# The second layer's bias of a mixture of experts: one stacked fp32r product a tile instead of a fp32 product, in two banks and two halves

## What is computed

```python
logits = xf @ gate_w + gate_b
top_v, top_i = jax.lax.top_k(logits, TOP_K)
top_w = jax.nn.softmax(top_v, axis=-1)
cw = jnp.zeros((T, NUM_EXPERTS)).at[jnp.arange(T)[:, None], top_i].add(top_w)
for e in range(NUM_EXPERTS):
    h = jax.nn.relu(xf @ w1[e] + b1[e])
    y = h @ w2[e] + b2[e]
    out = out + cw[:, e:e + 1] * y
```

## Time and profile before

| what | value |
|---|---|
| median of three runs | 1293.33 us |
| the profiled execution | 1289.2 us |
| its span | 1287.5 us |
| mean granted clock of PE | 0.988 |
| PE busy / PEld busy | 1246.4 / 1161.5 us |
| DVE busy / ACT busy / POOL busy | 842.4 / 675.0 / 159.2 us |
| the eight instructions of L1161 | 979.1 to 982.75 us |

### The profile page before, as it was taken

One profiled execution on the slowest core, in us unless ns is written; L12 is line 12 of the kernel. 1 busy time (PEld: TensorE's weight loads), 2 busy tenths in 40 slices (PEclk: granted clock), 3 DMA queues, 4 the chain that ended last, 5 costly groups with the idle time before them and its releaser, 6 DMA issues.

```text
span 1287.5 us, 22172 instructions
## 1 busy us (share of the span) xinstructions
PE 1246.4 (97%) x8497; PEld 1161.5 (90%) x8497; DVE 842.4 (65%) x2186; ACT 675.0 (52%) x1193; POOL 159.2 (12%) x86
## 2 busy tenths in 40 slices
PE   7999999999999999999999999999878999999997
PEld 6799999999999999999999999988767988989996
DVE  4556656566565666556566566685576788877877
ACT  5345545535544553464455455354444676767673
POOL 2203101300400220040031013000021000000012
PEclk9999999999999999999999999999969999999999
DMA  9002200310220040022022003100226667677763
GB/s 329 27 1 88 82 1 1 118 52 1 91 79 2 27 142 1 1 91 79 2 90 80 1 7 143 38 2 7 97 74 241 226 240 254 238 240 250 230 220 114
DMA packets 61506, 129.04 MB, mean 100 GB/s; under 512 B 3572, under 2 KB 21120, under 8 KB 61160
## 3 DMA queue, kind: packets, MB, share of 16 engines
q1 hardware_dynamic: 59240, 120.85, 27.4%
q0 software_dynamic: 2176, 6.95, 1.6%
HBM read 121.89 MB, written 15.34 MB: 107 GB/s over the span
## 4 chain that ended last, share of the span: by engine, by line
PE 92%; DVE 4%; ACT 2%; DMA 1%; issue 1%; POOL 0%; SPq 0%; POOLq 0%; DVEq 0%
PE ptp L830 24%; PE work L830 20%; PE work L1128 8%; PE pv L975 7%; PE ptp L959 7%; PE work L868 6%; PE work L1130 4%; PE ptp L1149 2%; PE ptp L1152 2%; PE ptp L1151 2%; PE ptp L1153 2%; PE ptp L1150 2%; PE work L837 2%; PE ptp L837 1%; DVE pt L1379 1%; DMA raw<-in_ctxT 1%
## 5 line engine op out<-in xcount | busy, mean ns | idle before, releaser
L830 PE MATMUL ptp<-vw_hi,cx_hi 128*128 128x256 f32 x832 | 241.8, 291 | 0.0
L830 PE MATMUL ptp<-vw_lo,cx_hi 128*128 128x256 f32 x832 | 235.4, 283 | 0.0
L830 PE MATMUL ptp<-vw_hi,cx_lo 128*128 128x256 f32 x832 | 235.4, 283 | 0.0
L518 POOL TENSOR_TENSOR cx_lo<-raw,cx_hi 128x1664 fp32r<-128x1664 f32 x30 | 113.8, 3792 | 666.3 <-ACT cx_hi L578 666.3
L830 PE MATMUL work<-cx_hi,kw_hi 128*128 128x400 f32 (+1 forms) x504 | 175.5, 348 | 2.9 <-POOL cx_lo L518 1.7
L830 PEld LDWEIGHTS ptp<-vw_hi,cx_hi 128*128 128x128 f32 x832 | 159.3, 191 | 17.0 <-issue 17.0
L830 PE MATMUL work<-cx_hi,kw_lo 128*128 128x400 f32 (+1 forms) x504 | 173.6, 345 | 0.0
L830 PE MATMUL work<-cx_lo,kw_hi 128*128 128x400 f32 (+1 forms) x504 | 173.2, 344 | 0.0
L1379 DVE TENSOR_TENSOR pt<-ptp,pt 128x512 fp32r<-128x512 f32 (+1 forms) x224 | 141.3, 650 | 33.3 <-ACT pt L578 29.8
L830 PEld LDWEIGHTS ptp<-vw_lo,cx_hi 128*128 128x128 f32 x832 | 159.3, 191 | 0.0
L830 PEld LDWEIGHTS ptp<-vw_hi,cx_lo 128*128 128x128 f32 x832 | 159.3, 191 | 0.0
(11 more groups left out here) (268 smaller groups left out, 2384.9 us busy)
## 6 DMA issues: line engine op xcount, KB each, us to landing
w1raw<-in_w SPq DMA_DIRECT2D x32, 1024.0 KB, 5.1
w2raw<-in_w SPq DMA_DIRECT2D x32, 1024.0 KB, 6.9
raw<-in_ctxT SPq DMA_DIRECT2D x31, 832.0 KB, 6.3
pr<-in_mask SPq DMA_DIRECT2D x8, 800.5 KB, 4.4
xrow<-x_rows SPq DMA_DIRECT2D x7, 256.0 KB, 6.2
y_rows<-y_out_rows POOLq DMA_DIRECT2D x7, 256.0 KB, 2.4
xin<-in_x SPq DMA_DIRECT2D x1, 1024.0 KB, 8.9
qwraw<-in_qwT SPq DMA_DIRECT2D x1, 1024.0 KB, 11.1
```

The lines of the kernel that those rows point to most:

```text
L518: pool.tensor_tensor(cx[1][:, :, sl], raw[:, k % 2], cx[0][:, :, sl].bitcast(F32), ALU.subtract).then_inc(c_lo, 1)
L830: last = pe.matmul(dst, lhs(i, c), rhs(j, c), start=(c == 0 and (i, j) == (0, 0)), stop=(c == n - 1 and (i, j) == (1, 0)))
```

## The change

`b2s` and `cwT` become fp32r and get 96 rows instead of 8. Three groups of 8 rows are used, at rows 0, 32 and 64; the others meet zeros in `cwT`. The weights side is high, low, high (of `cw`), the bias side high, high, low (of `b2`), so one product over 96 rows gives high x high + low x high + high x low.

For this b2 is loaded twelve times (into 96 rows), ACT makes the high part of all 96 rows, and DVE replaces rows 64 to 71 by the low part. DVE splits `cw` into `cw_k` (128 tokens x 96, zeroed by POOL), which PE turns instead of `cw`. The four products go by turns into `yb[2]` and `yb[3]`, two ahead of `second(0, 0, 0)` and two behind it, and `second(0, 0, 0)` no longer waits for `y_out`; the wait for all four additions is in front of piece 2, where `yb[2]` and `yb[3]` are used again.

```diff
+BK = 96
+B_HI, B_LO, B_HI2 = slice(0, E), slice(32, 32 + E), slice(64, 64 + E)
-            sp.dma_start(b2s[:], b2).then_inc(ld2[5], 16)
+            for i in range(BK // E):
+                sp.dma_start(b2raw[i * E:(i + 1) * E, :], b2).then_inc(ld2[5], 16)
+            pool.memset(cw_k[:], 0.0).then_inc(base_done, 1)
             act.activation(wts[:, 1], wts[:, 0], ACT.Exp).then_inc(gate_exp, 1)
+            act.wait_ge(ld2[5], 16 * (BK // E))
+            copy(b2s[:], b2raw[:], b2_hi)
@@ second
-                    if isinstance(n, int) and n == 0:
-                        pe.wait_ge(y_out, TT)
-                    elif ph:
+                    if ph:
                         pe.wait_ge(y_lo, ST * scattered(ph, e))
-                    else:
+                    elif not isinstance(n, int) or n:
@@ biases of PE
-            def biases():
+            def biases(ts):
                 pe.wait_ge(cwT_done, 1)
-                pe.wait_ge(ld2[5], 16)
-                for t in range(TT):
-                    pe.matmul(yb[t][:], cwT[:, t * P:(t + 1) * P], b2s[:], start=True, stop=True).then_inc(m_full, 1)
+                pe.wait_ge(b2_lo, 1)
+                for t in ts:
+                    if t >= 2:
+                        pe.wait_ge(y_out, t - 1)
+                    pe.matmul(yb[2 + t % 2][:], cwT[:, t * P:(t + 1) * P], b2s[:], start=True, stop=True).then_inc(m_full, 1)
@@ turn_rows
-                pe.wait_ge(cw_done, 1)
+                pe.wait_ge(cw_done, 3)
-                    last = pe.transpose(yb[3][0:E, t * P:(t + 1) * P], cw[:, t], ident[:])
+                    last = pe.transpose(yb[3][0:BK, t * P:(t + 1) * P], cw_k[:, t], ident[:])
@@ expert of PE
+                    if p == 2 and isinstance(n, int) and n == 0:
+                        pe.wait_ge(y_out, TT)
-                        biases()
+                        biases(range(0, 2))
                     second(ph, e, p)
+                    if p == 0 and isinstance(n, int) and n == 0:
+                        biases(range(2, TT))
@@ DVE
-                    dve.tensor_tensor(xs[:, t], xs[:, t], yb[t][:], ALU.add).then_inc(y_out, 1)
+                    dve.tensor_tensor(xs[:, t], xs[:, t], yb[2 + t % 2][:], ALU.add).then_inc(y_out, 1)
-            dve.tensor_tensor(cw[:], cw[:], cw2[:], ALU.add).then_inc(cw_done, 1)
+            dve.wait_ge(base_done, 2)
+            step(dve.tensor_tensor(cw[:], cw[:], cw2[:], ALU.add))
+            join()
+            step(dve.tensor_copy(cw_hi[:], cw[:]))
             dve.tensor_scalar(crowded[:], total[:, 0:1], float(SLOTS), None, ALU.is_gt).then_inc(flag_done, 1)
+            join()
+            dve.tensor_copy(cw_k[:, :, B_HI], cw_hi[:].bitcast(F32)).then_inc(cw_done, 1)
+            dve.tensor_copy(cw_k[:, :, B_HI2], cw_hi[:].bitcast(F32)).then_inc(cw_done, 1)
+            dve.tensor_tensor(cw_k[:, :, B_LO], cw[:], cw_hi[:].bitcast(F32), ALU.subtract).then_inc(cw_done, 1)
-            dve.tensor_copy(cwT[:], yb[3][0:E, :]).then_inc(cwT_done, 1)
+            dve.tensor_copy(cwT[:], yb[3][0:BK, :]).then_inc(cwT_done, 1)
+            dve.wait_ge(b2_hi, 1)
+            dve.tensor_tensor(b2s[B_HI2], b2raw[B_HI2], b2s[B_HI2].bitcast(F32), ALU.subtract).then_inc(b2_lo, 1)
```

More of the change, by code:

```diff
@@ L241, in layer @@
             b1r = sb(m, "b1r", [P, P], F32)
-            b2s = sb(m, "b2s", [E, D], F32)
+            b2raw = sb(m, "b2raw", [BK, D], F32)
+            b2s = sb(m, "b2s", [BK, D], F32R)
             w1raw = sb(m, "w1raw", [P, 2, C, 512], F32)
@@ L277, in layer @@
             cw2 = sb(m, "cw2", [P, TT, E], F32)
-            cwT = sb(m, "cwT", [E, T], F32)
+            cw_hi = sb(m, "cw_hi", [P, TT, E], F32R)
+            cw_k = sb(m, "cw_k", [P, TT, BK], F32)
+            cwT = sb(m, "cwT", [BK, T], F32R)
             placeT = sb(m, "placeT", [E, T], F32)
@@ L342, in layer @@
         y_hi, y_lo, y_put = sem("output_hi"), sem("output_lo"), sem("output_scattered")
+        b2_hi, b2_lo = sem("second_bias_hi"), sem("second_bias_lo")
         cw_done, cwT_done = sem("expert_weights_ready"), sem("expert_weights_transposed")
```

## The result

The changed kernel takes 1295.15 us (median of 20 runs, 1293.29 to 1297.58), the kernel before beside it 1293.13 us (20 runs, 1288.69 to 1295.13). The ratio is 1.0018, with a 95% interval from 1.0011 to 1.0025: 2.3 us slower by the ratio (the two medians lie 2.0 us apart), where +0.6 us was forecast. That is inside the range and still within 0.2%, but at its edge. Run again beside three variants, the same kernel gave 1.0020 (1.0007 to 1.0032), 2.6 us.

What follows compares the result with a forecast made beforehand. PE, carrying 92% of the chain of waits, was taken as the bound. A remaining gain of 0.7 us plus 1.3 us of low clock gave +0.6 us, median 1293.33 to 1293.9; the 8-in-10 range was 1291.3 to 1296.3.

Steps and rivals of the forecast that it cites:

- the preparations in cover: Eleven more loads, memset, ACT's copy, DVE's split of `cw`, PE's wider turn: all priced at 0, hidden in idle time.
- The low part of b2: On DVE between `cwT` and the row numbers: 0.60 us added on the path, so `hidden(0, 1)` starts later.
- The product: Bias products on PE: each stacked fp32r product over 96 rows takes 0.23 us, with bounds 0.23 and 0.43.
- The rival with 0.45: Bias products on PE: the stacked product runs at 0.45, not the fp32r rate, 0.65 us in all; chance 0.04.
- The full clock in `second(0, 0, 0)`: `second(0, 0, 0)` follows the bias products without a wait and takes 4.60 us at full clock; 1.65 us gained by clock.
- The new wait ahead of `hidden(0, 2)`: PE waits for DVE, whose third addition needs the later product: 3.7 us without any matmul; 0.7 us of gain remain.
- C: Ahead of `hidden(0, 2)`: DVE doesn't hold PE up, whole gain stays, 1288.7 us; chance of over 2.6 us gained 0.10.
- The clock behind the new wait: At `hidden(0, 2)`: the granted clock falls after PE's wait, costing 0 to 2.1 us, taken as 1.3.
- Case A: At `hidden(0, 2)`: PE waits for DVE and the clock falls, +0.1 to +1.4 us; the forecast, chance 0.52.
- B: At `hidden(0, 2)`: PE waits but the clock holds, -0.7 us, 1292.6; chance 0.26.
- The stretch ahead of `hidden(0, 1)`: PE's wait there grows from 2.2 to 2.8 us by DVE's added 0.60 us; no clock fall in the forecast.
- D: Clock falls twice, also in `hidden(0, 1)` after the longer wait: +2.7 to +3.1 us, 1296.2; chance 0.08.

Runs made afterwards that it cites:

- longer step: Kernel before plus one DVE subtraction of 8x512 values behind its copy of `cwT`, into a tile nobody reads; 1.0001 of before.
- product alone: Changed kernel with the old places: all four fp32r products ahead of `second(0, 0, 0)`, which waits for the four additions; 0.9991 of before.
- late additions: Changed kernel with DVE adding bias tiles 2 and 3 after the low parts of hidden piece 1; 0.9966 of before.
- filled wait: Changed kernel plus 16 PE products with zeros behind the fourth bias product, to fill the wait ahead of `hidden(0, 2)`; 1.0013 of before.
- filled ahead: Changed kernel, bias tiles 2 and 3 added later, b2's low part made before the turned rows, 9 unused PE products behind them; 0.9948 of before.

## Why the prediction was right, and where its size was off

- **What bounds the kernel, and the preparations in cover.** Right. What changes in this stretch reaches the end: the span without the part from the start of `hidden(0, 0)` to that of `second(0, 1)` is 1258.9 to 1261.1 us in all fourteen profiles, while that part went from 23.3 to 33.6. The twelve loads took 4.71 us of SyncE's queue, ACT's copy lay in idle time, and the split of `cw` ended at 967.5. The transposes of 96 columns took as long as those of 8 (0.60 us for four).
- **The low part of b2.** Right: 0.71 us against 0.60, and the longer step alone makes no more than 1.3 us in the timed runs.
- **The product.** Right: 0.24 to 0.26 us apart, over 96 rows. The rival with 0.45 falls.
- **The full clock in `second(0, 0, 0)`.** Right: 4.55 us against 6.25. It comes from the wait that is gone, not from the kind of product ("product alone", 6.26).
- **The new wait ahead of `hidden(0, 2)`.** Right in place, length and cause: 3.70 us, and moving two additions in DVE's list takes it away with 7.0 us. The other side, C, falls.
- **The clock behind the new wait.** Case A against B is decided, but the term was mis-sized: 1.3 us was taken of at most 2.1, and it was 2.5, 2.95 and 2.4 us in the three profiles. The bound came from a restart with 4.2 us of low clock; here it stayed low for 6.8 us. What it costs is half of what is left of the low stretch when PE starts again: from 992.86 to 998 in the first profile, 5.2 us, so 2.6, and 2.5 was measured. This term is 1.3 us too small on average. The Trainium skill (TensorE: Matmul & The Clock Gate, Why this matters for your kernels) warned of just such gaps, and the trace agrees with 0.61 and 0.50 in the windows from 991. The section speaks of gaps longer than the 2.20 us ahead of 974.36, so the full clock in the window of 973 didn't speak against it, as the prediction had it.
- **The stretch ahead of `hidden(0, 1)`.** Priced at +0.6 us with the clock unchanged. Wrong: every profile of the changed kernel has two falls, which is D's picture, and D had a chance of 0.08. D's cause, the longer wait, isn't needed for a fall: the second profile of before has one behind 2.20 us, and "late additions" has none behind 3.04. But the length of the low stretch goes with the wait at this place. Behind 2.20 to 2.33 us (seven profiles) it was 3.4 us in five and 0 in two; behind 3.04 us and more (seven) it was 6.8 us in six and 0 in one. So the price was 1.7 to 2.8 us in the changed kernel against 0 and 1.6 before.

As a sum by profiles: from the start of `hidden(0, 0)` to that of `second(0, 1)` before took 27.8 and 29.1 us and the changed kernel 33.6, 32.9 and 33.5, so 3.8 to 5.8 us more, where the ratios of the timed runs say 2.3 to 2.6. Against the profile that it started from, the forecast of +0.6 us is 5.2 us short: 1.2 of them are the clock behind the new wait, 2.25 the wait ahead of `hidden(0, 1)` (5.05 instead of 2.8, with the late copy) and 1.75 the low clock in it.

That the median still fell into the range is in part luck. The profiled execution of before, 1289.2 us, was a fast one: of the twenty timed beside the changed kernel only one was faster. The prediction said that none of its terms depended on this, but the second profile of before, 1291.57 us, has a fall that the first has not. Where those twenty lost the other microseconds (their median is 1293.13) no profile shows. What the record does show is that the times scatter with the granted clock: of the 26 runs of before beside "filled wait", nine with a mean clock of 0.987 have a median of 1292.08 us, and nine with 0.988 one of 1289.70. So the sizes rest on the ratios, and the profiles only on which term is there.

**Open.** In five of the fourteen profiles DVE was late with `placeT` or `cwT` after PE's turn: by 2.0 to 2.3 us (changed kernel twice, product alone), and in two steps, 0.9 to 1.3 and then 0.75 to 0.77 us, in "longer step" and "filled ahead". In each it went on 0.6 to 0.8 us behind the start of the last burst of token rows that POOL scatters. None of the four profiles in which DVE's list is as before at that place shows it. Whether it belongs to the added instructions or to the scatter was not settled, so the 2.0 to 2.2 us that it adds to the changed kernel's wait ahead of `hidden(0, 1)` have no known cause. They cost less than that, since a part of the low stretch then passes under the wait: the stretch of the sum took 33.6 and 33.5 us with them and 32.9 without.

## What to carry to other kernels

When work is taken off the engine that bounds, look at what the other engines' lists do with the time: here DVE's additions stood in front of the weights that PE needed next, and a later product made them late. Move the consumer with the producer; the same change then went from 1.0018 to 0.9966. And a wait of PE can cost more than its length, since the clock is low behind it: 3.7 us of wait cost 1.7 to 2.95 us more here. Last, one profile shows one execution: the kernel before had the clock at 1.00 in `hidden(0, 1)` in one and at 0.50 for 3.4 us in the other.

## What the hardware showed

- A wait of 3.3 to 3.7 us of PE was followed by 1.7 to 2.95 us lost at 1.2 GHz in all five profiles that had it; one of 2.2 to 2.3 us lost 0 or about 1.5 us, and one of 3.04 us 0 or 2.8 us, by the execution.
- Products with a stationary side of zeros held the clock at 1.00 in place of such a wait, in the one profile that has them.
- A fp32r product of 512 columns took 0.23 to 0.26 us with 96 rows, the fp32 one with 8 rows 0.86 to 0.96, in two instructions.
